# Four-layer convolution chain on one core: hat transfers, copies and products by groups of three taps

## The reference, cut to what matters

```python
om = _conv2d(x, w_off, b_off)
offset = om[:, :2 * KK]
mask = jax.nn.sigmoid(om[:, 2 * KK:])
py = off_y + hh[None, None, :, None] + ky[None, :, None, None] - PAD
px = off_x + ww[None, None, None, :] + kx[None, :, None, None] - PAD
sampled = jax.vmap(_bilinear_sample_one)(x, py, px)
sampled = sampled * mask[:, None]
out = jnp.einsum('bckhw,ock->bohw', sampled, w_dcn.reshape(O, C, KK))
```

## Time and profile before

| | us |
|---|---|
| median of 3 runs (280.73 to 282.88) | 281.18 |
| the profiled execution | 282.63 |
| its span in the profile | 280.8 |
| PE busy | 252.6 |
| DVE busy | 204.7 |
| ACT busy | 184.1 |
| POOL busy | 53.3 |

### The profile page before, as it was taken

How to read it: one execution, slowest core, us unless ns; L and a number is a source line. 1 busy time by engine, 2 the same in 40 slices (tenths; PEclk the granted TensorE clock), 3 DMA queues, 4 the chain that set the end, 5 groups by cost and what they waited for, 6 DMA issues and landing times.

```text
span 280.8 us, 7247 instructions
## 1 busy us (share of the span) xinstructions
PE 252.6 (90%) x2796; PEld 167.5 (60%) x2796; DVE 204.7 (73%) x353; ACT 184.1 (66%) x391; POOL 53.3 (19%) x99
## 2 busy tenths in 40 slices
...
GB/s 233 204 0 176 242 284 272 322 245 287 280 294 270 240 297 267 241 304 281 258 259 251 248 247 268 268 283 253 244 259 256 110 19 22 2 2 0 9 30 19
DMA packets 22881, 56.47 MB, mean 201 GB/s; under 512 B 4160, under 2 KB 6464, under 8 KB 22720
## 3 DMA queue, kind: packets, MB, share of 16 engines
...
...
## 4 chain that ended last, share of the span: by engine, by line
PE 51%; DVE 17%; ACT 13%; issue 9%; POOL 8%; ACTq 0%; DVEq 0%; POOLq 0%
PE ps_cv L497 11%; PE ps_quad L579 5%; PE ps_quad L482 5%; PE ps_m L444 5%; DVE sb_wt L868 5%; POOL sb_sc L1012 2%; PE ps_quad L571 2%; PE ps_m L467 2%; PE ps_quad L601 2%; ACT sb_xe L712 2%; PE ps_m L559 2%; DVE sb_b_max L875 2%; PE ps_m L511 2%; ACT sb_gates L774 2%; PE ps_quad L536 2%
## 5 line engine op out<-in xcount | busy, mean ns | idle before, releaser
L868 DVE TENSOR_TENSOR sb_wt<-sb_wt,sb_xe 128x1024 f32<-128x1024 f32 x72 | 87.9, 1233 | 11.7 <-ACT sb_xe L712 11.5
L497 PE MATMUL ps_cv<-sb_wt,sb_w_x 128*64 128x256 f32 x576 | 74.9, 388 | 5.3 <-DVE sb_wt L868 4.4
L497 PEld LDWEIGHTS ps_cv<-sb_wt,sb_w_x 128*64 128x64 f32 x576 | 40.2, 138 | 27.5 <-DVE sb_wt L868 7.9
L712 ACT ACTIVATE sb_xe<-sb_xe 64x512 f32<-64x512 f32 x72 | 44.8, 627 | 3.4 <-ACT sb_hats L686 1.6
L1009 POOL TENSOR_SCALAR sb_sc<-sb_mv 128x1 f32<-128x1 f32 x16 | 9.8, 612 | 116.6 <-DVE sb_mv L940 64.1
L910 DVE SCALAR_TENSOR_TENSOR sb_dw_acc<-sb_z_pad,sb_par,sb_dw_acc 128x256 f32<-128x256 f32 x56 | 23.0, 479 | 6.8 <-ACT sb_dw_acc L762 6.8
L482 PE MATMUL ps_quad<-sb_par,sb_x 64*128 64x256 f32 (+1 forms) x192 | 24.3, 378 | 0.8 <-ACT sb_w_x L703 0.6
L1002 POOL COPY sb_x<-sb_x_pad 128x256 f32<-128x256 f32 x8 | 6.3, 787 | 92.6 <-PE ps_quad L482 57.4
L774 ACT ACTIVATE sb_gates<-ps_quad,sb_gate_bh 128x512 f32<-128x512 f32 x16 | 10.1, 681 | 17.0 <-PE ps_quad L579 17.0
L703 ACT ACTIVATE sb_w_x<-ps_quad 128x1024 f32<-128x1024 f32 (+1 forms) x24 | 19.0, 807 | 3.0 <-PE ps_quad L482 1.8
L482 PEld LDWEIGHTS ps_quad<-sb_par,sb_x 64*128 64x128 f32 x192 | 16.7, 197 | 6.8 <-issue 5.7
...
## 6 DMA issues: line engine op xcount, KB each, us to landing
sb_wt<-hat_rows SPq DMA_DIRECT2D x144, 256.0 KB, 10.3
sb_xe<-hat_rows SPq DMA_DIRECT2D x72, 128.0 KB, 9.7
...
sb_x_in<-in_x SPq DMA_DIRECT2D x8, 128.0 KB, 6.0
out_y<-sb_x_in SPq DMA_DIRECT2D x8, 128.0 KB, 1.7
...
```

The lines of the kernel that those rows point to most:

```text
L497: mm = nc.tensor.matmul(cv[C * b:C * (b + 1), 0:PIX], w_x[n % 2][:, b, h, k, :], wt[slot(n, k)][:, h, PIX * b:PIX * (b + 1)], start=(k == ...
L712: nc.scalar.activation(xe[i][C:P, :], xe[i][0:C, :], ACT.Copy).then_inc(ev("dup_ok"), 1)
L868: nc.vector.tensor_tensor(wt[i][:, :, :], wt[i][:, :, :], xe[i][:, :].unsqueeze(1).to_broadcast([P, HALVES, 2 * PIX]), ALU.mult)\
```

## The change

`get`, `d` and `w` now handle a group of three taps at once. The transposed rows are stored in another order (position first, then tap), so that each partition reads one contiguous run: 6 KB for `xe`, 12 KB for `wt`. There are four slots of three taps in place of nine of one. SyncE issues 72 transfers for 216, ScalarE 24 copies of 1536 elements for 72 of 512, VectorE 24 products of 3072 elements for 72 of 1024. TensorE's samples stay 72, each of four matmuls, and wait for the product of their group.

Other edits come with it. The slots need room, so `nrm` writes over `b_exp`, `prod` over `conv` and `u` over `ff_g`, each with a wait for the earlier pair's reader. One plus the mask is computed by GpSimd (`msk`) and no longer inside `hat_y`. The factor of the logits goes into q, and `max` returns the negated maximum in one instruction. A norm on GpSimd has four steps in place of five. All five lists in `PLAN` and the counts of idle matmuls are new.

```diff
-RING = 9
+SLOTS = 4
-HOT = {1: 15, 2: 5, 3: 11, 4: 9, 5: 10, 6: 4, 7: 10, 8: 8}
-WARM = {1: 5, 2: 3, 3: 3, 4: 2, 5: 3, 6: 2}
+HOT = {1: 5, 2: 5, 3: 2, 4: 7, 5: 10, 6: 11, 7: 8, 8: 8}
+WARM = {1: 5, 2: 3, 3: 3, 4: 3, 5: 3, 6: 3}
-        hat = sb("hat", [P, 4, AXES, H])
+        hat = sb("hat", [P, 4, GROUPS, 2, H * OF_GROUP])
-        xe = [sb(f"xe{i}", [P, 2 * PIX]) for i in range(RING)]
-        wt = [sb(f"wt{i}", [P, HALVES, 2 * PIX]) for i in range(RING)]
+        xe = [sb(f"xe{i}", [P, OF_GROUP, 2 * PIX]) for i in range(SLOTS)]
+        wt = [sb(f"wt{i}", [P, HALVES, OF_GROUP, 2 * PIX]) for i in range(SLOTS)]
...
+            def get(g):
+                def step(n):
+                    sp.wait_ge(rows_out[n % 2][g], 16 * ((n + 1) // 2))
+                    wait_past(sp, ev("smp_mm"), OF_GROUP * (group(n, g) - SLOTS))
+                    i = slot(n, g)
+                    sp.dma_start(xe[i][0:C, :, :].rearrange("p t q -> p (t q)"),
+                                 rows[n - 1, g, ROWS // 2:ROWS, :].rearrange("(x t) q -> x (t q)", t=OF_GROUP).unsqueeze(1)
+                                 .to_broadcast([W, RUN, OF_GROUP * 2 * PIX])).then_inc(slot_x[i], 16)
                     for j in range(2):
+                        a = ROWS // 4 * j
+                        sp.dma_start(wt[i][C * j:C * (j + 1), :, :, :].rearrange("p h t q -> p (h t q)"),
+                                     rows[n - 1, g, a:a + ROWS // 4, :].rearrange("(y k) q -> y (k q)", y=RUN).unsqueeze(0)
+                                     .to_broadcast([W, RUN, HALVES * OF_GROUP * 2 * PIX])).then_inc(slot_in[i], 16)
...
-                    pe.wait_ge(ev("wt_ok"), tap(n, k))
+                    pe.wait_ge(ev("wt_ok"), group(n, k // OF_GROUP))
...
+                    act.wait_ge(slot_x[i], filled(n, g))
+                    nc.scalar.activation(xe[i][C:P, :, :], xe[i][0:C, :, :], ACT.Copy).then_inc(ev("dup_ok"), 1)
...
+                    dve.wait_ge(slot_in[i], 2 * filled(n, g))
+                    dve.wait_ge(ev("dup_ok"), group(n, g))
+                    nc.vector.tensor_tensor(wt[i][:, :, :, :].rearrange("p h t q -> p h (t q)"),
+                                            wt[i][:, :, :, :].rearrange("p h t q -> p h (t q)"),
+                                            xe[i][:, :, :].rearrange("p t q -> p (t q)").unsqueeze(1)
+                                            .to_broadcast([P, HALVES, OF_GROUP * 2 * PIX]), ALU.mult).then_inc(ev("wt_ok"), 1)
...
+            def msk_step(n):
+                pool.wait_ge(ev("tanh_ok"), n)
+                wait_past(pool, ev("hat_y_ok"), n - 1)
+                nc.gpsimd.tensor_scalar(msk1[:, :, :], msk[:, :, :], 1.0, 1.0, ALU.add, ALU.mult).then_inc(ev("msk_ok"), 1)
...
-                    nc.gpsimd.tensor_tensor(scl[:, 2:3], scl[:, 1:2], col(gain, 0), ALU.mult).then_inc(ev(g_ok), 1)
+                    nc.gpsimd.tensor_tensor(scl[:, 2:4], both[:, :], scl[:, 1:2].to_broadcast([P, 2]), ALU.mult)\
+                        .then_inc(ev(g_ok), 1)
                     pool.wait_ge(ev(g_ok), n)
-                    nc.gpsimd.tensor_tensor(scl[:, 4:5], src_mv[:, 0:1], scl[:, 2:3], ALU.mult).then_inc(ev(m_ok), 1)
-                    pool.wait_ge(ev(m_ok), n)
-                    nc.gpsimd.tensor_tensor(scl[:, 3:4], col(gain, 1), scl[:, 4:5], ALU.subtract)\
+                    nc.gpsimd.tensor_scalar(scl[:, 4:5], src_mv[:, 0:1], scl[:, 3:4], col(gain, 1), ALU.mult, ALU.add)\
```

More of the change, by code:

```diff
@@ L78 @@
+        s0.8 s1.8 logit.7@p0 et1.6@m1 s2.8 ff.4@p1 av.6@m1 s3.8 s4.8 s5.8 ff2.4@m1 gs.5@p0+p1 s6.8 s7.8 s8.8 et0.7@m1
+        et1.7@m2 qk2.8@m0 av.7@m2 gs.6@p0+p1 v2.8@m2 fuse.5@m0 hot.1 logit.8@p0 fuse.6@m2 ff.5@p1 hot.2 et0.8@m2 hot.3
+        et1.8@m0 ff.6@p1 ff2.5@m2 av.8@m0 hot.4 ff2.6@m0 gs.7@p0+p1 hot.5 gs.8@p0+p1 fuse.7@m0 hot.6 fuse.8@m0 ff.7@p0
+        hot.7 ff2.7@m0 ff.8@p0 hot.8 ff2.8@m0
     """,
     "act": """
-        attn.1 at.1 mix.1 attn.2 attn.3 at.2 halve.1 off.1 wx0.1 prep.1 wx2.1 tanh.1 abs.1 wx1.1 mix.2 at.3 tr0.1 tr1.1
@@ L86 @@
-        k2.2 wx0.4 tanh.7 v2.2 d2.3 exp0.1 exp1.1 d3.3 exp0.2 d4.3 wx2.4 exp1.2 d5.3 tr0.6 tr1.6 put0.6 d6.3 et0.1 et1.1
-        put1.6 tr2.6 abs.7 d7.3 put2.6 et0.2 et1.2 d8.3 at.8 ln1.1 dw.1 d0.4 tr0.7 relu.3 wx0.5 d1.4 q2.3 k2.3 d2.4
-        wx1.5 wx2.5 v2.3 d3.4 ln1.2 put0.7 dw.2 tr1.7 gate.1 d4.4 scan.1 d5.4 put1.7 tr2.7 mix.8 put2.7 d6.4 exp0.3 d7.4
-        exp1.3 d8.4 et0.3 ln2.1 d0.5 et1.3 d1.5 relu.4 wx0.6 wx1.6 d2.5 ff.1 off.8 ln1.3 d3.5 dw.3 gate.2 d4.5 scan.2
-        q2.4 k2.4 d5.5 wx2.6 d6.5 v2.4 d7.5 d8.5 exp0.4 exp1.4 ln2.2 d0.6 tanh.8 d1.6 et0.4 et1.4 abs.8 d2.6 relu.5 d3.6
@@ L96 @@
-        ff.6 gate.8 ln2.7 scan.8 ff.7 ln2.8 ff.8
+        attn.1 at.1 attn.2 mix.1 attn.3 at.2 at.3 halve.1 mix.2 off.1 wx0.1 wx1.1 prep.1 mix.3 tanh.1 wx2.1 abs.1 off.2
+        wx0.2 tr1.1 tr2.1 put2.1 tr0.1 put0.1 put1.1 tanh.2 abs.2 wx2.2 wx1.2 attn.4 off.3 tr2.2 put2.2 tr1.2 tr0.2
+        put0.2 tanh.3 put1.2 abs.3 attn.5 at.4 mix.4 attn.6 tr2.3 tr1.3 put2.3 tr0.3 put0.3 d0.1 off.4 put1.3 at.5 at.6
+        mix.5 mix.6 tanh.4 abs.4 d1.1 attn.7 off.5 tr2.4 tr1.4 put2.4 put1.4 tr0.4 put0.4 d2.1 tanh.5 abs.5 off.6 at.7
@@ new lines @@
+        mix.7 d0.2 tanh.6 relu.1 wx1.3 wx0.3 q2.1 k2.1 wx2.3 tr1.5 v2.1 tr2.5 put2.5 put1.5 exp0.1 exp1.1 d1.2 et0.1
+        tr0.5 put0.5 et1.1 abs.6 attn.8 d2.2 ln1.1 dw.1 off.7 at.8 mix.8 d0.3 relu.2 wx2.4 wx1.4 q2.2 k2.2 wx0.4 v2.2
+        d1.3 exp0.2 exp1.2 tr1.6 tanh.7 tr2.6 put2.6 put1.6 tr0.6 d2.3 et0.2 et1.2 put0.6 abs.7 off.8 d0.4 ln1.2 relu.3
+        dw.2 wx0.5 tr1.7 wx1.5 d1.4 q2.3 k2.3 tr2.7 put2.7 put1.7 gate.1 scan.1 v2.3 tanh.8 d2.4 gate.2 scan.2 abs.8
+        d0.5 wx2.5 exp0.3 ln2.1 exp1.3 relu.4 wx0.6 ff.1 et0.3 d1.5 ln2.2 q2.4 k2.4 tr0.7 ff.2 put0.7 et1.3 d2.5 exp0.4
```

231 lines of the change are left out of this document (106 added, 125 removed).

## The result

| | before | after |
|---|---|---|
| median | 281.06 us (4 runs) | 306.51 us (4 runs, 305.98 to 307.26) |
| span of the profiled execution | 280.8 | 304.3 |
| ratio of the times | | 1.0893 (95% interval 1.0839 to 1.0947) |

A forecast was written before the change was run, and what follows sets the result against it. The prediction took hat transfers into SBUF, at 241 GB/s, to bound the kernel. Its terms, -2.0 + 5.5 - 3.7 - 0.8 = -1.0 us, took the profiled 282.63 to 281.6, so the median to 280, range 268 to 293.

The forecast's parts named there:

- What bounds the kernel: Middle stretch: hat transfers never stop, at 241 GB/s; the way into SBUF limits them, each get writing half the partitions.
- Rival D: End of the stretch: engines set it, not transfers, so some engine work comes off; 273 to 277 us, chance 0.16.
- Term 3: Rate of the hat transfers in the stretch: taken as unchanged, no gap charged.
- The sign that I had set for B: SP queue's rate between first and last get: under 234 GB/s would speak for the rival of a falling rate.
- Rival B: Hat transfers: the rate falls to 228 GB/s as engines stay longer in one half; +10, 290 us, chance 0.24.
- The stretch of 216 us: Hat transfers at the skill's ceiling of about 218 GB/s for partitions 0 to 63: 20 us more.
- Term 2: Start of the stretch: reordered convolution, transposes and first put delay the first group; +5.5 us, bounds +2 and +8.
- Term 4: Last group: 6.3 us from last landing through product and three samples, before 10.0; -3.7 us, bounds -5 to +1.
- Term 5: ScalarE's copies 1.48 us each, VectorE's products 3.4; -9.3 and -7 us of work, worth nothing in the stretch.
- Terms 6 and 7: GpSimd norms and softmax maximum: -0.5 and -0.3 us; end after the last sample: 0, bounds -3 and +4.
- Term 1: Transfers: 216 gets become 72 with the same bytes; -2.0 us, bounds nothing and 4 us.
- Rivals C and E: Larger transfers run faster, 266 to 274 us, chance 0.12; three taps at once stall the engines, 287 us, chance 0.12.

The follow-up runs named there:

- the transfers out of the way: The changed kernel with its large transfers, but from pair 3 on without those to partitions 64 to 127: 279.17 us, ratio 0.9954.
- the order alone: The kernel before, its per-tap transfers issued three taps at a time, three in a row to each half of the partitions: 300.56 us, ratio 1.0713.
- cut kernel: The changed kernel, each group's transfers cut into the nine of before: median 281.0 us in four runs, 284.3 in eight more (ratio 0.9859).

## Why the prediction was wrong

- *What bounds the kernel.* Wrong. I read a queue that never runs dry as a limit. It never runs dry because nine slots are asked for as soon as they are free. The rows that spoke against it were used for something else: at 7.4 us from issue to landing, with 2.7 us a tap, some three of nine slots are under way and the others have landed and wait (around 90 us, at 18.5, it was seven). The kernel with two fifths of the hats' bytes left out from pair 3 on takes as long (1.0005). Rival D had this for the end of the stretch; the 273 to 277 us that it made of it did not come even with the transfers out of the way (279.2).
- *Term 3, "Taken as unchanged".* This is the step that failed, and it carries the miss: 217.5 GB/s instead of 241, +21.3 us. The sign that I had set for B, a rate under 234, came. Rival B had the mechanism, "an engine's stay in one half grows threefold", and the order alone, in the kernel before, costs 19.8 us. B's size was too small (228 GB/s, +10): it let a third of the gain over 220 stay, and nothing stayed. The stretch of 216 us that I had set beside it, from the 218 GB/s of the Trainium skill, is near the 218.8 us measured. I gave B 0.24 against 0.36 on the ground that engines might stay apart by packets; no row supported that.
- *Term 2, start +5.5*: 28.75 for 23.67, +5.1. Right, with its parts a little off: 3.6 us to the first copy of `hats` (20.94 to 24.51) where 4.4 were summed, and 1.5 behind it where 1.0 were.
- *Term 4, last group -3.7*: -2.4. From the last landing to the last sample's end 7.6 us pass, not 6.3: between the product's end (250.9) and the three samples (252.30) TensorE ends gate and scan of another pair.
- *Term 5*: 3.38 and 1.48 us measured, 3.4 and 1.48 said. Right, and worth almost nothing, as said; the reason given ("the transfers hide them") is half of it.
- *Terms 6 and 7, -0.8 and 0*: -0.4 for the end as a whole. Right within half a microsecond.
- *Term 1, -2.0 for 144 transfers fewer.* Nothing shows it. The cut kernel has them all again and its best run, 275.8, is below the best without the limit, 276.7.
- *Rivals C and E.* Large transfers ran no faster. Granularity showed no loss on balance: 0.9954 with it and without the transfers' limit.

Without the fall of the rate the sum looks good: it said 281.6, and the cut kernel took 281.0 and 284.3 in its two sets. That is in part luck. The sets mix executions at different rates, and the one at 243 GB/s, next to the 241 of the sum, took 288.7, 7 us more. Its stretch was 195 us long, as summed, but its last sample ended 13.7 us behind the last landing, where term 4 had 6.3: the credit for the quick handing over seems to hold only where the transfers come as slowly as in the changed kernel (7.6 us). No kernel here is clearly faster than the one before; the changed one would need its transfers at 258 GB/s in every run, and even then would gain one to two per cent at most (an estimate from 278.1 us in the execution at 258 GB/s and 275.8 in the quickest, for 280.8 and 280.5 before).
